# Normalised input in a ring of three and an image's response scale spread over three steps

## The reference, cut to what matters

```
# layer 0: shifted windows of 7 x 7, 3 heads
xn  = layernorm(x) over channels                # per pixel: (x - mu) * rsqrt(var + 1e-5) * g + b
xw  = windows of roll(xn, -3, -3)               # 256 windows of 49 tokens per image
att = softmax(q k / sqrt(16) + relative bias)
x   = x + unroll((att v) @ proj_w + proj_b)
x   = x + gelu(layernorm(x) @ fc1_w + fc1_b) @ fc2_w + fc2_b

# layer 1: depthwise 7 x 7 convolution, then global response normalisation
y  = layernorm(depthwise_conv7(x) + dw_b)       # over channels
y  = gelu(y @ w1.T + b1)                        # 192 features
gx = sqrt(sum(y * y over the whole image))      # per image and feature
nx = gx / (mean(gx over features) + 1e-6)
y  = grn_g * (y * nx) + grn_b + y
x  = x + y @ w2.T + b2
```

## Time and profile before

| | |
|---|---|
| profiled execution | 2077.34 us |
| its span, first to last instruction | 2075.7 us |
| median of the 3 runs | 2073.83 us |
| busy, of the span | TensorE 86%, ScalarE 75%, VectorE 73%, GpSimd 57% |
| mean granted TensorE clock | 0.946 of 2.4 GHz |
| DMA | 262.18 MB, 126 GB/s over the span |

### The profile page before, as it was taken

The page is one execution under the profiler, slowest core; times in us unless marked ns, Lnnn a source line. Parts: engine busy times, 40 slices in busy tenths (PEclk is TensorE's granted clock), DMA queues, the critical chain, the costliest instruction groups (busy, mean ns, idle before and its releaser), DMA issues. The chain is left out here.

```text
span 2075.7 us, 90932 instructions
## 1 busy us (share of the span) xinstructions
PE 1777.1 (86%) x38074; PEld 1065.6 (51%) x38074; DVE 1508.5 (73%) x2014; ACT 1550.2 (75%) x2882; POOL 1174.7 (57%) x1048
## 2 busy tenths in 40 slices
PE   4989898989888898989898989874999959889884
PEld 2655555555555555555555555531788823223321
DVE  7687777878777777787777777534777757767772
ACT  3788888888888888888888888763566658777770
POOL 4676767777776767676767777731455611111121
PEclk9999999999999999999999999985899957889998
DMA  4334544343434343434434343312587769899983
GB/s 106 80 101 106 146 104 115 91 115 87 119 84 118 86 118 87 109 96 105 100 97 109 93 112 83 93 32 56 155 216 211 203 128 197 218 217 211 242 200 105
DMA packets 233223, 262.18 MB, mean 126 GB/s; under 512 B 167078, under 2 KB 179910, under 8 KB 232710
## 3 DMA queue, kind: packets, MB, share of 16 engines
q1 hardware_dynamic: 217478, 217.50, 43.1%
q0 software_dynamic: 15360, 39.08, 6.6%
HBM read 160.82 MB, written 80.88 MB: 116 GB/s over the span
## 5 line engine op out<-in xcount | busy, mean ns | idle before, releaser
L415 POOL TENSOR_TENSOR shift<-const_b,qmax 113x588 bf16<-113x588 bf16 x256 | 345.8, 1351 | 55.1 <-DVE qmax L510 54.9
L440 POOL TENSOR_TENSOR xl<-x 113x784 bf16<-113x784 f32 x64 | 136.7, 2136 | 263.8 <-DVE x L532 263.8
L1475 POOL DMA_DIRECT2D out_rolled<-r_OUT x128 | 64.3, 504 | 319.5 <-DVE r_OUT L1577 316.4
L510 DVE TENSOR_REDUCE qmax<-ps_s 113x12 f32<-113x588 f32 x256 | 194.7, 760 | 63.0 <-PE ps_s L890 63.0
L496 DVE TENSOR_TENSOR xh<-X,RS 113x784 f32<-113x784 f32 x64 | 229.1, 3580 | 2.9 <-DMA RS<-rs_scratch 2.1
L731 ACT ACTIVATE G<-ps_m 128x392 f32<-128x392 f32 x384 | 184.1, 498 | 50.9 <-PE ps_m L992 50.1
L699 ACT ACTIVATE P<-ps_t 113x588 f32<-113x588 f32 x256 | 171.9, 672 | 54.2 <-PE ps_t L942 53.5
L1323 PE MATMUL conv_ps<-xin,band_now 64*64 64x448 bf16 x2688 | 203.1, 364 | 4.1 <-DVE x_low L1225 4.1
L405 POOL TENSOR_TENSOR xhl<-xh 113x784 bf16<-113x784 f32 x64 | 203.4, 3178 | 2.2 <-DVE xh L550 2.2
L692 ACT COPY Uf<-ps_m 113x392 f32<-113x392 f32 x384 | 172.8, 485 | 30.9 <-PE ps_m L857 22.6
L502 DVE TENSOR_TENSOR Ul<-Uf 113x784 bf16<-113x784 f32 x192 | 182.6, 977 | 0.0
(11 more groups left out here) (240 smaller groups left out, 5267.3 us busy)
## 6 DMA issues: line engine op xcount, KB each, us to landing
xin<-rows_scratch SPq DMA_DIRECT2D x96, 236.0 KB, 3.8
XT<-x_tokens SPq DMA_DIRECT2D x64, 294.0 KB, 4.6
X<-x_windows SPq DMA_DIRECT2D x128, 147.0 KB, 2.9
RS<-rs_scratch SPq DMA_DIRECT2D x128, 147.0 KB, 3.4
XR<-x_windows SPq DMA_DIRECT2D x128, 147.0 KB, 3.7
x_scratch<-x SPq DMA_DIRECT2D x128, 147.0 KB, 3.9
y_scratch<-y POOLq DMA_DIRECT2D x96, 196.0 KB, 2.8
r_RS<-rs_scratch SPq DMA_DIRECT2D x128, 147.0 KB, 3.8
```

Source lines behind the costliest of these rows:

```text
L415: nc.gpsimd.tensor_tensor(shift[:, j % 2], e, m, ALU.mult).then_inc(S["md"], 1)
L440: nc.gpsimd.tensor_tensor(xl1[:], x1[:, r, :], x1m[0][:, r, :], ALU.subtract).then_inc(S["x1_lo"], 1)
L510: nc.vector.tensor_reduce(qmax[:, j % 2, :].rearrange("p (b n) -> p b n", b=2), ps_s[0:R, :, 0:2 * HQ].rearrange("p b (n t) -> p b n t", t ...
```

## The change

In attention, xh0 and xl0 become rings of three (HRING). `normalise0` of strip s+2 moves from near the end of VectorE's step to its first half, before `first_residual`, and waits for the scores of strip s-1 in place of those of s. `low0` moves from the end of GpSimd's step to before `x1_low`. SP's step begins with the loads of X and RS, `swap_halves` comes third, and `residual_load` after the stores of x2.

In response, LAG grows to 11, and G's ring shrinks to 14. The scale of an image is made in three consecutive steps, in columns of ps_m, which `fc1`'s third part uses, and no longer of ps_o: sums of pairs in one step, the mean in the next, the scaled weights in the third; the addition of epsilon moves from VectorE to ScalarE (`keep_mean`). `sum_squares` on VectorE runs one step sooner. `fc1(s, t)` waits for the GELU of the same part of the strip before, where it waited for all three parts. X2 has a ring of three and is loaded one step before its use, ahead of RS and Y. The loop with a register is gone: every step is written out.

```diff
+HRING = 3
-        xh0 = sb("xh0", [R, 2, STRIP])
-        xl0 = sb("xl0", [R, 2, STRIP], BF16)
+        xh0 = sb("xh0", [R, HRING, STRIP])
+        xl0 = sb("xl0", [R, HRING, STRIP], BF16)
...
             def step(s, image):          # SP, attention
-                swap_halves(s.at(1))
                 x_load(s.at(2))
                 rs_load(s.at(2))
-                residual_load(s)
+                swap_halves(s.at(1))
                 tokens_load(s.at(TLEAD))
                 x2_store(s.at(-3), image)
+                residual_load(s)
                 rs_store(s.at(3))
...
                 make_shift(s, 2)         # GpSimd, attention
+                low0(nx2)
                 x1_low(prv)
...
                 squares_low(prv)
-                low0(nx2)
...
-                    wait(dve, S["st"], 4 * (s.n - 1))      # normalise0
-                    nc.vector.tensor_tensor(xh0[:, r, :], X[:, r, :], RS[:, r, :], ALU.mult).then_inc(S["xh0"], 1)
+                    wait(dve, S["st"], 4 * (s.n - 2))
+                    nc.vector.tensor_tensor(xh0[:, s.slot(HRING), :], X[:, r, :], RS[:, r, :], ALU.mult).then_inc(S["xh0"], 1)
...
                 divide(prv, 3)           # VectorE, attention
+                normalise0(nx2)
                 first_residual(prv)
...
                 divide(s, 1)
-                normalise0(nx2)
                 query_max(nxt, 1)
...
-        RING = 2 * STRIPS
-        LAG = STRIPS + 2
+        RING = STRIPS + 6
+        SLOTS = 2 * STRIPS
+        LAG = STRIPS + 3
+        XRING = 3
...
-                nxt, old = s.at(2), s.at(-LAG)       # SP, response
+                nxt, old = s.at(2), s.at(1 - LAG)
+                if old.real:
...
+                    wait(sp, S["out_made"], old.n - XRING + 1)
...                                                  # X2 here, then RS and Y; X2 stood last
...
             def step(s):                 # VectorE, response
                 nx2 = s.at(2)
-                respond(s.at(-LAG))
-                sum_squares(s.at(-2))
-                add_up(s.at(-LAG + 1))
+                sum_squares(s.at(-1))
+                add_up(s.at(-STRIPS))
                 finish(s.at(-LAG))
+                respond(s.at(-STRIPS - 2))
                 normalise(nx2)
...
             def step(s):                 # ScalarE, response
                 features(s, 0)
                 features(s, 1)
-                norms_root(s.at(-LAG + 1))
                 features(s, 2)
+                keep_mean(s.at(-STRIPS - 1))
+                norms_root(s.at(-STRIPS))
                 sum_squares(s)
...
-                        wait(pe, S["ge"], 3 * (s.n - 1) + 1)      # fc1
-                    elif t == 1:
-                        wait(pe, S["ge"], 3 * s.n)
+                    wait(pe, S["ge"], 3 * (s.n - 1) + t + 1)
+                    if t == 2 and s.raw >= STRIPS:
+                        wait(pe, S["gx_made"], (s.raw - 1) // STRIPS)
+                        wait(pe, S["mean_made"], (s.raw - 2) // STRIPS)
...
                 old = s.at(-LAG)         # TensorE, response
                 fc1(s, 0)
-                respond(old, 1)
-                respond(old, 2)
                 fc2(old)
                 fc1(s, 1)
+                mean_of_norms(s.at(-STRIPS - 1))
+                pair_sums(s.at(-STRIPS))
                 fc1(s, 2)
-                respond(s.at(-LAG + 1), 0)
```

More of the change, by code:

```diff
@@ L1414, in response_phase @@
         S = sems("cleared y_cleared setup_v setup_t f1 f2 pairs mean_ps xh summed summed_act totals "
-                 "gx_made inv_made scaled w2_scaled out_made ge lo")
+                 "gx_made mean_made inv_made scaled w2_scaled out_made ge lo")
         y_loaded = [sem(f"r_y_loaded{r}") for r in range(2)]
-        x2_loaded = [sem(f"r_x2_loaded{r}") for r in range(2)]
+        x2_loaded = [sem(f"r_x2_loaded{r}") for r in range(XRING)]
         stored = [sem(f"r_stored{r}") for r in range(2)]
@@ L1425, in halves, with steps @@
             return ap.rearrange("p (b n) -> p b n", b=2)
[L1427 to L1436, removed]
+        def steps(step, last):
+            for raw in range(-2, last):
                 step(Strip(0, raw, N))
@@ L1444, in step @@
             def step(s):
-                nxt, old = s.at(2), s.at(-LAG)
+                nxt, old = s.at(2), s.at(1 - LAG)
+                if old.real:
+                    if old.n == 0:
+                        wait(sp, S["cleared"], CLEARS)
+                    wait(sp, S["out_made"], old.n - XRING + 1)
+                    for g in range(2):
+                        sp.dma_start(X2[ROWB * g:ROWB * g + C, old.slot(XRING), :],
+                                     by_strip[0][old.n // STRIPS, old.n % STRIPS, g]
+                                     ).then_inc(x2_loaded[old.slot(XRING)], 16)
                 if nxt.real:
@@ L1454, in step @@
                                      ).then_inc(y_loaded[r], 16)
[L1455 to L1464, removed]
+            steps(step, N + LAG)
         @block.gpsimd
@@ L1479, in step @@
                 store(s.at(-LAG))
-            steps(pool, step, N + LAG)
+            steps(step, N + LAG)
             for r in range(2):
@@ L1495, in _ @@
                 nc.vector.memset(t[:], 1.0).then_inc(S["y_cleared"], 1)
+            nc.vector.memset(eps1[:], EPS1).then_inc(S["y_cleared"], 1)
             dve.wait_ge(S["cleared"], CLEARS)
@@ L1552, in respond @@
                 if s.real and s.raw % STRIPS == 0:
[L1553 to L1557, removed]
+                    img, p = s.raw // STRIPS, s.raw // STRIPS % 2
+                    wait(dve, S["mean_made"], img + 1)
+                    wait(dve, S["scaled"], 2 * img)
                     nc.vector.reciprocal(inv[:], mean[:]).then_inc(S["inv_made"], 1)
-                    wait(dve, S["inv_made"], 2 * img + 2)
+                    wait(dve, S["inv_made"], img + 1)
+                    wait(dve, S["w2_scaled"], 2 * img)
                     nc.vector.scalar_tensor_tensor(out=scale[:], in0=gx[:], scalar=inv[:, 0:1], in1=grn_g[:],
@@ L1624, in step @@
                 features(s, 1)
-                norms_root(s.at(-LAG + 1))
                 features(s, 2)
+                keep_mean(s.at(-STRIPS - 1))
+                norms_root(s.at(-STRIPS))
                 sum_squares(s)
-            steps(act, step, N + LAG)
+            steps(step, N + LAG)
         @block.tensor
@@ L1694, in fc2 @@
                     slot = s.raw % RING
+                    if s.raw % STRIPS == 0:
+                        wait(pe, S["w2_scaled"], 2 * (s.raw // STRIPS) + 2)
                     wait(pe, S["out_made"], s.n)
@@ L1712, in step @@
                 fc1(s, 0)
-                respond(old, 1)
-                respond(old, 2)
                 fc2(old)
                 fc1(s, 1)
+                mean_of_norms(s.at(-STRIPS - 1))
+                pair_sums(s.at(-STRIPS))
                 fc1(s, 2)
-                respond(s.at(-LAG + 1), 0)
-            steps(pe, step, N + LAG)
+            steps(step, N + LAG)
 def constants():
```

84 lines of the change are left out of this document (47 added, 37 removed).

## The result

| | before | after |
|---|---|---|
| median (4 runs each) | 2072.76 us | 2044.62 us (2039.60 to 2049.31) |
| profiled execution | 2077.34 us | 2049.31 us |
| its span | 2075.7 us | 2047.6 us |

The ratio is 0.9862, with a 95% interval from 0.9836 to 0.9889: 1.4% faster; 2038 us was forecast. The terms did not all come out, and two of the errors cancel. In the profile of after the lines are normalise0 L497, low0 L398, u_low L503, first_residual L533, x1_low L441, low1 L406 and fc1 L993 in attention, and in response finish L1572, normalise L1522, fc1 L1679, fc2 L1713 and L1719, features L1609, the root L1618.

What follows compares the result with a forecast made beforehand. The prediction took TensorE to bound attention (worth 0) and X2's load and the response scale's chain, with DMA close behind, to bound response. From the 2073.83 us median, 35.6 us less in response gave 2038 us, range 2028 to 2048.

Steps and rivals of the forecast that it cites:

- Attention 0 (±2): Attention: moved xh0 and low0 are hidden in idle time, worth 0; the phase's start and end move by at most 2 us.
- What is behind them in the two queues therefore starts as before: Attention: after the moved xh0 and low0, later work on VectorE and GpSimd keeps its times, xhl's 0.94 us wait included.
- X2's wait goes, and DMA is late next, 4.61 us a strip: Response: finish's 0.70 us a strip waiting for X2 goes; then 1.204 MB at 261 GB/s sets 4.61 us a strip.
- rival (b): Response: DMA is no limit, engines set 4.34 us a strip, 24 us less, 2014 us; chance 0.10.
- The sentence on the Trainium skill: Response DMA: about 358 GB/s of HBM per core would give an estimated 3.4 us a strip; the forecast kept the measured rate.
- 1.5 us left per boundary: Response, image boundary: its cost of 4.25 us per image falls to 1.5, bounded by 0 and 4.25.
- No step over about 6.5 us: Response, sign that the forecast is right: no step at the image boundaries longer than about 6.5 us.
- The two table loads are no longer in the chain to fc2: Response boundary: ScalarE's two table loads (2.6 us) now sit in a chain with nearly a step's slack.
- 4.80 us a strip: Response: 4.61 us for DMA plus 1.5/8 for the boundary, where a strip took 5.36 us; ends 4.15 and 5.2.
- Strip 0 one microsecond later: Response start: LAG 11 finishes strip 0 one step later but without the chain before it, taken as +1 us.
- Sum of response: Response: 1 + 52 * 4.80 + 11 * 3.61 = 290.3 us against 325.9 before, difference -35.6 us.
- Rival (c): Attention: it gains too, up to 53 us, if the changed order lets xhl start before Ul; 1985 to 2034 us; chance 0.05.

## Why the prediction was right, point by point

- **Attention 0 (±2).** The mechanism held: xh0, low0, the step and the hole before fc1 are as written. The size did not: attention ends 6.7 us later in the profile, and its part alone costs 5 to 11 us. Of the 6.7 us, 2.7 lie ahead of the first fc1, where the other profiles differ by 3 us whichever order they have; 4.1 us lie in the steps. The step that failed is "What is behind them in the two queues therefore starts as before": it does in nearly all steps, but at step 34 the 0.06 us by which xhl starts first are lost, and the clock falls behind the hole.
- **X2's wait goes, and DMA is late next, 4.61 us a strip.** The first half is right (no r_X, 12.7 us for r_Y). The second is wrong: single steps run at 4.15 us, a whole stretch at 4.43 without the table loads. 261 GB/s was what the transfers did under that load, not what they could do: in after they reach 303 GB/s for 4 us. This was rival (b). The sentence on the Trainium skill ("DMA: Bandwidth & Descriptors", Specifications, about 358 GB/s for a core) pointed that way; the stretches shown here stay under its figure.
- **1.5 us left per boundary.** Too small. With a quarter less traffic and no wait for r_Y a strip takes 4.65 us; that is 0.50 over TensorE's 4.15, 4.0 us per image, of which the table loads make 2.0. "No step over about 6.5 us" failed: three of six boundaries take 7.8. "The two table loads are no longer in the chain to fc2" missed that they hold up the GELUs, and that fc1 waits for these, at three boundaries with the clock as its price (0.57 over 4 us in the one shown, as before). And 8.40 us was one boundary of six; their mean before is 8.87.
- **4.80 us a strip.** 4.74 measured. It is right by luck: 0.46 us too much for DMA stands against 0.3 too little for the boundary, and a wait for r_Y that is partly hidden.
- **Strip 0 one microsecond later.** It is 4.1 us later against the end of attention (10.8 less 6.7), and 4.2 with response's part alone, a whole step of 4.15: the chain that goes from in front of it saved nothing there. The end stretch took 40.89 us for 39.7.
- **Sum of response:** 287.18 us from strip 0 to 63 plus 4.1, against 325.93: -34.7, where -35.6 was forecast. That is one profile against one. By the medians of the runs beside each other response's part alone is worth 30 us (27 to 33), so that it stands at 2043.43 us without any cost in attention, and the two parts, 0.9856 and 1.0038, make 0.9894 together, just outside the interval of the whole change. In which phase the 6 us between 2038 and 2044.62 were lost is therefore not shown: the profiles say attention, the medians response. A sum read from one execution has an error of that size: from strip 0 to 63 the response of before takes 325.93 us in the profile that the prediction used, and 321.93 to 329.10 us in the four other profiles that have it unchanged.

Rival (c), that attention holds 53 us in the wait for xhl, was right about the place and wrong about this change: a different order gets 35 of them.

## What to carry to other kernels

A DMA share of 1.0 or more did not say here that transfers set the time: take bytes away, and see whether the engine that computes does more in the same stretch. To move an instruction that another engine holds up gains nothing if the critical engine waits for a different one; look for the instruction that is late in front of the critical engine, and move what runs beside it. A chain that is spread over more steps is free only if each of its pieces is; a table load of 1.28 us on ScalarE, which has 0.4 us to spare in a step of 4.15, is not. When TensorE is left waiting, read the granted clock of the next few us as well: the hole of 1.63 us in attention cost 0.7 us in its own step and 3.4 in the next.

## What the runs showed that was not expected

- xhl on GpSimd starts 0.06 us ahead of Ul and yet ends behind both (3.26 us; 2.38 beside one Ul, 1.49 alone); when it starts 0.28 us behind the first Ul it gets in between them (2.22 us, and 3.33 for the pair instead of 1.85). At one step of after it starts 0.72 us ahead, takes 1.49 us, and the pair takes 2.49. The Trainium skill ("SBUF — State Buffer", Who interferes with whom) lets the one that issues first have the ports for the whole instruction. The second and the third case fit that for Ul and xhl in turn; in the first the start on record is not what decides.
- On GpSimd an operation on 128x2 numbers takes 0.19 us with 0.08 us to the next that depends on it, and 0.87 and 0.81 us for two of the chain, at the same shape; why these two are longer was not tried.
